# The variance of the last norm from two fp32r products of a split square

## The reference, cut to what matters

```python
def _layer_norm(x, gamma, beta):
    mu = jnp.mean(x, axis=-1, keepdims=True)
    var = jnp.var(x, axis=-1, keepdims=True)
    return (x - mu) * jax.lax.rsqrt(var + LN_EPS) * gamma + beta
...
out = jnp.einsum('ne,end->nd', w_dense, y).reshape(B, S, D)
out = _layer_norm(out + x, gamma, beta)
return out
...
t = t + _L1_ffn_ref(_ln_t(t), ...)
```

## Time and profile before

| | us |
|---|---|
| median of 3 runs (lowest to highest) | 2894.42 (2891.84 to 2895.83) |
| the profiled execution, its own time | 2892.19 |
| its span, first to last instruction | 2890.3 |
| last stage in it, about | 2500 to 2890 |
| mean granted TensorE clock, share of full speed | 0.962 |

### The profile page before, as it was taken

How to read it: one execution, slowest core, us unless ns; L and a number is a source line. 1 busy time by engine, 2 the same in 40 slices (tenths; PEclk the granted TensorE clock), 3 DMA queues, 4 the chain that set the end, 5 groups by cost and what they waited for, 6 DMA issues and landing times. The chain is left out here.

```text
span 2890.3 us, 42401 instructions
## 1 busy us (share of the span) xinstructions
PE 2646.8 (92%) x12188; PEld 1491.8 (52%) x12188; DVE 1492.8 (52%) x2823; ACT 1583.9 (55%) x2305; POOL 510.6 (18%) x408
## 2 busy tenths in 40 slices
PE   8976786999999999999999999999889999288887
PEld 4642344555555555555555555555467777133333
DVE  6632898344444444444444444443369998245545
ACT  5630565555555555555555555555456665266666
POOL 3320775000000000000000000000058887100000
PEclk9988897999999999999999999999989999599999
DMA  4467675434243433424333342433113232464552
GB/s 132 132 143 162 177 202 175 103 79 95 65 97 72 88 86 75 96 64 97 77 83 90 71 96 65 96 80 81 40 58 115 106 115 108 115 184 137 168 156 86
DMA packets 168940, 308.47 MB, mean 107 GB/s; under 512 B 50626, under 2 KB 161058, under 8 KB 161570
## 3 DMA queue, kind: packets, MB, share of 16 engines
q1 hardware_dynamic: 168866, 307.60, 41.6%
HBM read 210.12 MB, written 97.39 MB: 106 GB/s over the span
## 5 line engine op out<-in xcount | busy, mean ns | idle before, releaser
L781 ACT ACTIVATE hidden<-hidden_psum,b 128x896 f32<-128x896 f32 x896 | 854.5, 1004 | 707.0 <-PE hidden_psum L730 707.0
L847 DVE SCALAR_TENSOR_TENSOR weighted<-y_psum,b,w_bc 128x448 f32<-128x448 f32 x448 | 306.2, 684 | 925.1 <-PE y_psum L744 911.5
L744 PE MATMUL y_psum<-hidden,w 128*64 128x448 f32 x3584 | 773.4, 552 | 2.7 <-DVE weighted L847 2.7
L729 PE MATMUL hidden_psum<-tokens,w1hi 128*128 128x448 f32 x1792 | 706.3, 394 | 13.8 <-DMA ident<-in_ident 11.0
L730 PE MATMUL hidden_psum<-tokens,w1lo 128*128 128x448 f32 x1792 | 660.6, 369 | 0.0
L729 PEld LDWEIGHTS hidden_psum<-tokens,w1hi 128*128 128x128 f32 x1792 | 337.0, 188 | 333.3 <-ACT hidden L781 294.4
L744 PEld LDWEIGHTS y_psum<-hidden,w 128*64 128x64 f32 x3584 | 217.7, 136 | 351.0 <-issue 246.8
L730 PEld LDWEIGHTS hidden_psum<-tokens,w1lo 128*128 128x128 f32 x1792 | 338.2, 189 | 24.2
L198 ACT ACTIVATE ln_r<-ln_var,eps 128x448 f32<-128x448 f32 x280 | 177.7, 635 | 239.8 <-PE ln_var L183 135.9
L158 PE MATMUL ln_xc<-X,centre 128*128 (+1 forms) x448 | 226.4, 589 | 72.0 <-DVE X L608 53.1
L1043 POOL MEMSET pad_lo<- 128x116 f32 (+1 forms) x4 | 0.8, 267 | 1592.7 <-POOLq L665 1592.7
(11 more groups left out here) (128 smaller groups left out, 2450.8 us busy)
## 6 DMA issues: line engine op xcount, KB each, us to landing
w_bc<-scr_wtok SPq DMA_DIRECT2D x112, 896.0 KB, 10.5
tokens<-scr_split SPq DMA_DIRECT2D x224, 224.0 KB, 3.7
scr_split<-hi SPq DMA_DIRECT2D x112, 224.0 KB, 2.0
scr_split<-lo SPq DMA_DIRECT2D x112, 224.0 KB, 1.9
scr_xn<-xn SPq DMA_DIRECT2D x56, 224.0 KB, 2.0
tokens_plus_y<-scr_xn SPq DMA_DIRECT2D x56, 224.0 KB, 2.6
out<-out_tile SPq DMA_DIRECT2D x56, 224.0 KB, 2.0
X<-in_x SPq DMA_DIRECT2D x6, 1792.0 KB, 7.6
```

What stands on the lines that cost most here:

```text
L729: pe.matmul(o, w1hi[:, s * P:(s + 1) * P], S[:, b, a, :], start=True, stop=False)
L744: mm = pe.matmul(yp[C * a:C * a + C, e % 2, 0:TW], w2[:, e, c, :], hs[:, s % (2 * CH0), a, :], start=(c == 0), stop=(c == CH0 - 1))
L781: act.activation(hs[:, k % (2 * CH0)], hp[:, k % 2, :, 0:TW], ACT.Gelu, bias=b1[:, e, c:c + 1])\
L847: dve.scalar_tensor_tensor(out=pr[:, e % 2], in0=yp[:, e % 2, 0:TW], scalar=b2[:, e:e + 1], in1=WB[:, b, e, :], op0=ALU.add, op1=ALU.mult) ...
```

## The change

The last norm is built with `split`. Its averaging matrix is copied once to fp32r on ScalarE, PE waits for that copy once, GpSimd gets a program of 56 differences (7 for each pair), and `act_square` and `pe_var` take their other branch.

```diff
-            ln = Norm(ctx, "ln5", 4, 2, group=KT, xc=xc)
+            average_r = sbuf(ctx, "average5_r", [P, P], F32R)
+            average_ready = sem(ctx, "p7_average")
+            ln = Norm(ctx, "ln5", 4, 2, group=KT, xc=xc, split=average_r)
...
+                @block.gpsimd
+                def _(pool):
+                    def pair(p, b, last):
+                        for k in range(KT):
+                            ln.pool_square_lo(pool, KT * p + k, k)
+
+                    every_pair(pool, pair)
+
                 @block.tensor
                 def _(pe):
+                    pe.wait_ge(average_ready, 1)
...
                 @block.scalar
                 def _(act):
+                    act.activation(average_r[:], AVG[:], ACT.Copy).then_inc(average_ready, 1)
```

## The result

| | before | after |
|---|---|---|
| median of the runs (us) | 2893.13 (4 runs, 2891.16 to 2895.83) | 2918.88 (4 runs, 2916.05 to 2921.8) |
| profiled execution (us) | 2892.19 | 2916.05 |
| its span (us) | 2890.3 | 2914.1 |

The ratio is 1.0088, with a 95% interval from 1.0071 to 1.0106: slower by 25.7 us. The forecast was 2919, in a range from 2904 to 2934.

The account below looks back on a forecast made before the run. VectorE was taken as the bound, at about 1.92 us a tile. Slower norm parts add 17 us and the clock 9.4: 26.4 on 2892.2 gives 2918.6, forecast as 2919 for the median, range 2904 to 2934.

Parts of the forecast that it names:

- The loop over two tiles: Norm part: square, GpSimd's difference, variance and r with two buffers take 4.39 us per two tiles; +2.2 us a pair, 15.4 for seven.
- the start: Start of each norm part: two fp32r products reach r in 0.72 us instead of 0.95, saving 0.23 us a pair.
- the part from load to load: Norm part between ScalarE's table loads: expected to take 17.8 us or more, against 15.62 before.
- VectorE beside GpSimd: Norm part: g and the difference contend for SBUF; g comes first, GpSimd pays (1.37 us instead of 1.13), g stays 0.62.
- Rival 4: Norm part: VectorE loses to GpSimd each time, 2.45 us a tile, 3.0 a pair; 2926 us in all; chance 0.09.
- The last pair: Last norm part, with `finish` in it: VectorE remains the bound; 1.5 us, between bounds of -0.2 and 3.2.
- ScalarE's second square: Norm part: ScalarE needs 1.99 us a tile, just over VectorE's 1.92; alone it would cost 0.4 us a pair.
- The clock: TensorE's clock halves behind longer idle time: all seven turns fall, +6.9 us; one fall per norm part, +2.5; together +9.4.
- Rival 1: Norm parts slow as forecast, but the clock falls no more often than now: 2909 us; chance 0.19.
- Rival 2: Not slower: square to r within 2.27 us hides the wait behind VectorE's two steps; 2888 to 2894 us; chance 0.08.
- Rival 3: The clock stays low through most of each norm part, costing 27 us in place of 2.5; about 2943; chance 0.06.
- The page on precision: PE's variance: a true fp32 product is four passes against one reduced, so two fp32r products would cost half of it.

Follow-up runs that it names:

- The filled runs: Products nobody reads, added on PE where it idles: changed kernel 2902.99 us, kernel before 2887.57, changed kernel without GpSimd's difference 2888.3, fp32r products alone 2881.03.

## Why the prediction was right, point by point

**The loop over two tiles** is shown: 4.31 us against the 4.39 predicted, opened by taking the difference away (norm part 18.47), and bare where filling keeps the clock (4.32, 4.31, 4.31). Doubling the difference stretched it (5.6 at the least), though part of the 24.80 there is the clock's and VectorE's. The term was 2.2 us a pair, seven pairs 15.4. With the clock kept it measured 20.17 - 18.25 = 1.92, seven pairs 13.4 (18.25 is a norm part of the kernel before with a full clock). It came out a little smaller for two reasons. The difference took 1.30 us where it met g (29 of 56 instances) and 1.13 in nearly all others, 1.22 in the mean, where the prediction took 1.37 for all; and the start gained 0.35, not 0.23: first square to first r is 4.62 us after (2691.41 to 2696.03) and was 4.97 (2685.76 to 2690.73).

```profile
L173 POOL TENSOR_TENSOR ln_sq_lo<-ln_sq,ln_sq_hi 128x448 fp32r<-128x448 f32 x56 | 68.0, 1220 | 357.9 <-ACT ln_sq L166 357.9
L212 DVE SCALAR_TENSOR_TENSOR ln_g<-ln_q,ln_r 128x448 f32<-128x448 f32 x56 | 36.2, 647 | 1.9
```

One sign did not come: the part from load to load was to be 17.8 us or more. It is 17.35 to 18.07, and only one pair of seven reaches 17.8, since the loads moved against the squares (see the result). The expert parts, to be 30 us and over from load to load, took 30.5 to 31.9.

**VectorE beside GpSimd.** That g would come first and GpSimd pay is what the first seven norm parts show: all 49 g take 0.62 to 0.63 us, and the differences beside them 1.30 instead of 1.13. Rival 4 falls for these. The mean of 647 ns hides that it did not fall in the last pair, where `finish` shifts VectorE against GpSimd. There the difference of tile 4 began 0.05 us before g of tile 2:

```profile
2897.21 1.13 POOL L173 TENSOR_TENSOR ln_sq_lo<-ln_sq,ln_sq_hi 128x448 fp32r<-128x448 f32 x1 [1.00 <-ACT ln_sq L166]
...
2897.26 1.56 DVE L212 SCALAR_TENSOR_TENSOR ln_g<-ln_q,ln_r 128x448 f32<-128x448 f32 x1
```

So g took 1.56 us, and that of tile 3 took 0.91. With the difference doubled, 24 of the 49 g of the first seven pairs were lengthened as well. The order of arrival decides, as was argued from the earlier trace rows.

**The last pair** was put at 1.5, the middle of wide bounds, and is 1.8. The upper bound's reason is the one that held: the two long g and two lengthened `finish` steps (0.84 and 1.33 us for 0.68) took 2.0 us more than usual.

**ScalarE's second square** alone was put at 0.4 a pair. It cost 0.5 in the four norm parts whose clock stayed up (18.74 to 18.81) and 0.6 in the mean.

**The clock** was the term with the widest bounds: +9.4, of which 6.9 in the expert parts and 2.5 in the norm parts. Measured on the profiled executions it is 6.7 in the seven expert parts behind a turn, and in the norm parts what is left of their 16.9 without the pace, 3.5; together 10.2. Size and place were right: all seven turns fell. The reason given was right in part only. The prediction named less work on PE and a longer time ahead of each turn, and worked out the longer time: the hole that the wait for GpSimd opens, 1.33 us growing to 3.5 (it grew to 3.24). The falls did not need that hole. Without GpSimd's difference all seven turns fell, and six of seven norm parts had a low stretch; with the shorter products alone it was the same. Less work was enough: a variance keeps PE busy 0.67 us (2699.63 to 2700.30) where it was 0.99. What the hole changes is the price in the norm part: the low stretch costs 0.1 us a part without the difference (18.47 against 18.34 filled) and 0.6 in the changed kernel (20.78 against 20.17), where PE's products stand in the loop. The filled runs settle that it is the clock; how much work ahead of a turn keeps it was not measured.

**Rival 1**, with the clock falling no more often than before, falls by the expert parts (seven long ones, where three were). **Rival 2** needed the wait hidden behind VectorE's two steps, and q's idle time shows that it isn't. **Rival 3**, a low clock through most of each norm part, falls: one stretch in each, 0.6 us.

**What cancels.** Terms as measured give 13.4 + 1.8 + 10.2 = 25.4, and the sum predicted was 26.4. On the profiled executions pair 0 adds 1.4 and the earlier start of the stage takes 2.9, neither of which was shown to be the change's; that makes the 23.9. The medians differ by 25.7. That the median met the forecast to 0.1 us is chance: the single terms were off by up to 2 us, in both directions, and 2918.6 with the 2.2 that the prediction names is 2920.8, not 2919. The upper end of its range doesn't follow from its bounds either: the pace and the clock's upper bound make 2892.2 + 17 + 17 = 2926, not 2934. The copy of the matrix cost nothing that shows: PE's first product of the stage was still released by a DMA of weights, after 34.19 us of waiting (33.91 before).

**The page on precision.** The Trainium skill (FP8 and Floating Point Precision, section TensorE Precision Notes) makes a true fp32 product four passes. The rows agree more closely than the prediction's 0.72 for 0.95, which is the time to the end: two fp32 products behind each other take 1.67 us where one takes 0.99, so the second adds 0.7, while in the changed kernel fp32r products behind each other start 0.2 us apart (pair 3: 2695.63, 2695.82, 2696.03). Where nothing else changed the saving gave 0.5 to 0.7 us a norm part (17.90 against 18.37, and 17.57 against 18.26 with the holes filled). Of the 0.7, 0.35 came at the start, as argued, and the other half between the first r and the last (10.71 to 10.37), where the prediction had put it at nothing; in the changed kernel the loop hides that half.

## What to carry to other kernels

A step moved onto an idle engine is not free if it sits between two steps of a chain: write down the chain from one buffer's use to its next use, divide by the number of buffers, and compare that with the busiest engine's time per tile. An instance of the same chain elsewhere in the same trace gives the loop's length to a few per cent. And where a TensorE that waits for others gets less to do, look at what its clock did behind the holes that it already has: shorter products can lose by the clock what they save (the products alone took 2894.69 us against 2891.76, no measurable difference, and 2881.03 with the holes filled).

## What the runs showed of the hardware that was not expected

Added products that nobody reads made four kernels faster, since they keep the granted clock at 2.4 GHz over a wait: 14.6 to 15.9 us in the changed kernel, 11.9 without the difference, 13.7 with the products alone, and 4.2 in the kernel before. In the changed kernel, the price of half the clock was some 1.7 us for each expert part behind a turn (27.95 against 26.26), though only its first few microseconds ran at 1.2 GHz (behind pair 3: 0.50 from 2711 to 2717, 0.88 in the next 3 us, then 1.00). The falls came behind waits of PE that had left the clock alone when more work stood ahead of them (2.46 and 2.48 us).

VectorE's g and GpSimd's difference, both with two inputs in SBUF, lengthen each other by order of arrival: a lead of 0.05 us for GpSimd made g 1.56 us instead of 0.62, and g ahead of the difference made that 1.30 instead of 1.13.
